# Second attention with another order of units, and tile 0 of the first batch beside the first searched unit

## What is computed

```python
# per batch, Sq = 512, 32 query heads of 16, 8 key heads
draft = jnp.einsum('bhqd,bhkd->bhqk', qr, kr)        # rotated queries and keys
draft = draft + jnp.where(causal_future, neg, 0.0)
num_remain = 128
_, draft_indices = jax.lax.top_k(draft, num_remain)  # each row keeps its 128 largest
# softmax over those that are kept, times the values, then the output projection
```

## Time and profile before

| | |
|---|---|
| median of 3 runs | 2259.57 us (2258.46 to 2261.43) |
| the profiled execution | 2258.43 us |
| its span | 2256.6 us |
| PE, DVE, ACT, POOL busy | 1860.4, 1500.8, 1181.4, 802.9 us |
| the second attention's first score | 1160.4 us |
| its last residual addition | 2029.7 us |

### The profile page before, as it was taken

How to read it: one execution, slowest core, us unless ns; L and a number is a source line. 1 busy time by engine, 2 the same in 40 slices (tenths; PEclk the granted TensorE clock), 3 DMA queues, 4 the chain that set the end, 5 groups by cost and what they waited for, 6 DMA issues and landing times. The chain is left out here.

```text
span 2256.6 us, 27824 instructions
## 1 busy us (share of the span) xinstructions
PE 1860.4 (82%) x8600; PEld 1331.2 (59%) x8600; DVE 1500.8 (67%) x3325; ACT 1181.4 (52%) x2969; POOL 802.9 (36%) x523
## 2 busy tenths in 40 slices
PE   5898999988999769999765777778777777777997
PEld 4777777777777648887652443333444333335885
DVE  3677777777777644555652788888788888723335
ACT  3556656566565432333326677876677676242221
POOL 3445445455453435565321111112311112123442
PEclk9999999999999979999775778879887888887998
DMA  4011111111110112221240000010000000001111
GB/s 159 25 53 60 65 67 43 52 59 71 60 47 21 61 56 102 94 84 56 98 105 17 15 15 15 15 29 11 18 15 15 15 15 15 0 0 52 51 42 51
DMA packets 48722, 104.11 MB, mean 46 GB/s; under 512 B 6672, under 2 KB 30864, under 8 KB 44432
## 3 DMA queue, kind: packets, MB, share of 16 engines
q1 hardware_dynamic: 48624, 102.95, 13.7%
HBM read 95.59 MB, written 7.34 MB: 46 GB/s over the span
## 5 line engine op out<-in xcount | busy, mean ns | idle before, releaser
L225 PE MATMUL PS<-XT,AR 128*128 128x512 f32 x2472 | 620.2, 406 | 25.9 <-POOL AR L833 12.3
L225 PE MATMUL PS<-AR 128*128 128x512 f32 (+2 forms) x2568 | 540.7, 365 | 24.8 <-POOL AR L342 13.2
L225 PEld LDWEIGHTS PS<-XT,AR 128*128 128x128 f32 x2472 | 471.3, 193 | 139.4 <-issue 16.7
L225 PEld LDWEIGHTS PS<-AR 128*128 128x128 f32 x2568 | 441.5, 192 | 117.8 <-POOL AR L342 16.2
L1436 POOL TENSOR_TENSOR AF<-AF 128x512 f32<-128x512 f32 (+3 forms) x64 | 148.4, 2320 | 675.0 <-DVE AF L1668 675.0
L1610 DVE MAX8 BF<-PS 128x8 f32<-128x256 f32 (+2 forms) x384 | 196.7, 555 | 60.7 <-PE PS L1233 59.1
L1376 ACT ACTIVATE AF<-PS 128x512 f32<-128x512 f32 x160 | 92.5, 595 | 268.6 <-PE PS L1244 191.5
L1258 PE MATMUL PS<-AF,BF 128*128 128x512 f32 x320 | 190.3, 699 | 28.8 <-ACT AF L1376 28.6
L586 POOL TENSOR_TENSOR AF<-AF 128x512 f32<-128x512 f32 (+1 forms) x64 | 107.5, 1680 | 169.2 <-DVE AF L717 169.2
L580 POOL TENSOR_TENSOR AF<-AF 128x512 f32<-128x512 f32 x80 | 103.3, 1292 | 169.3 <-ACT AF L372 169.3
L1212 PE MATMUL PS<-AR,XT 48*128 48x128 f32 (+3 forms) x256 | 94.9, 454 | 73.3 <-DVE BF L1538 40.7
(11 more groups left out here) (195 smaller groups left out, 3451.2 us busy)
## 6 DMA issues: line engine op xcount, KB each, us to landing
AF<-in_mean_w SPq DMA_DIRECT2D x48, 448.0 KB, 3.3
AF<-in_ffn_w SPq DMA_DIRECT2D x14, 1536.0 KB, 6.6
AF<-in_attn_w SPq DMA_DIRECT2D x9, 1536.0 KB, 8.1
XT<-rope_scratch SPq DMA_DIRECT2D x180, 64.0 KB, 2.8
AF<-in_attn_w SPq DMA_DIRECT2D x9, 1024.0 KB, 5.0
AF<-in_ffn_w SPq DMA_DIRECT2D x11, 769.0 KB, 4.2
rope_scratch<-BF SPq DMA_DIRECT2D x20, 256.0 KB, 2.3
AF<-in_x SPq DMA_DIRECT2D x8, 256.0 KB, 4.1
```

Of the source, the lines that this page charges most:

```text
L225: last = nc.tensor.matmul(dst, lhs(a, c), rhs(m, c), start=(first and k == 0), stop=(k == 3 * n - 1 and not more))
```

## The change

The order becomes `TILES1 = [0, 1, 2, 3, 7, 6, 5, 4]`, and tile 0 is no unit any more: units now begin with tile 1, so there are 14 of them (`n = x // 2 + 1`), and step x picks and counts what step x + 2 did. The two halves e = 0, 1 of tile 0 are done by functions of their own with buffers of their own: `Se[e]`, columns 256 to 511 of the second score buffer, and `qe[e]` for the queries. Exponentials are made in place in `Se` (L1454), and all 16 heads are normed by one instruction.

```diff
-        NB = 2 * TT
-        TILES1 = [0, 1, 2, 3, 5, 6, 7, 4]
+        NB = 2 * (TT - 1)
+        TILES1 = [0, 1, 2, 3, 7, 6, 5, 4]
...
+        Se = [S1[1][:, :, 256 + P * e:256 + P * (e + 1)] for e in range(2)]
+        qe = [XT2[0:48].rearrange("p (h k) -> p h k", h=16), AR1[0:48, 4096:6144].rearrange("p (h k) -> p h k", h=16)]
...
+            def extra_scores(e):
+                pe.wait_ge(A1["qste"], 16 * 12)
+                pe.wait_ge(A1[f"kst{e}"], 48)
+                for pair in range(8):
...
+            def extra_values(e, g):
+                if g == 0:
+                    pe.wait_ge(A1["pnorm"], e + 1)
+                if g < 4:
+                    tn = 4 * e + g
+                    wait(pe, A1["pt"], tn - 1)
+                    for h in range(G1):
+                        last = nc.tensor.transpose(PS[:, 4 + tn % 2, h * P:(h + 1) * P], Se[e][:, 4 * g + h, :], ident)
...
                     if 0 <= xp - 1 < NB and h <= tile_of(xp - 1)[1] + 1:
                         values(xp - 1, 3, h)
-                    if h == 12 and xp >= 1 and (xp - 1) % 2:
-                        project((xp - 1) // 2)
+                    if x == 1 and 4 <= h <= 8:
+                        extra_values(0, h - 4)
+                    if h == 12 and xp >= 2 and (xp - 1) % 2:
+                        project((xp - 1) // 2 + 1)
+                    if h == 12 and x == 2:
+                        project(0)
...
+                if x == 1:
+                    for g in range(5):
+                        extra_values(1, g)
...
+            def extra_exp(e):
+                act.wait_ge(A1["nmax"], 2)
+                for h in range(16):
+                    last = nc.scalar.activation(Se[e][:, h, :], Se[e][:, h, :], ACT.Exp, bias=nmax_e[:, e, h:h + 1],
+                                                scale=SCALE1, accum_out=rsum_e[:, e, h:h + 1])
+                last.then_inc(A1["exp"], 1)
...
                 if x >= 3 and x % 2:
...
-                if shown:
+                    o_hi((x - 3) // 2 + 1, tcount(x - 1, 0, 0))
+                if x == 1:
+                    extra_pt(0)
+                    extra_exp(1)
+                elif shown:
                     exp(xp, 0)
                 if search:
                     count(x, 1)
+                if x == 0:
+                    extra_exp(0)
+                if x == 1:
+                    exp(0, 0)
                 if shown:
                     exp(xp, 1)
+                if x == 1:
+                    extra_pt(1)
+                    o_hi(0, 8)
                 if search:
                     count(x, 2)
...
+                if x == -1:
+                    first_thresholds()
                 for q in range(4):
                     if 0 <= xp < NB:
                         final(xp, q)
                     if x + 1 < NB:
                         evac(x + 1, q)
+                    if x == 0 and q == 2:
+                        extra_rinv(0)
+                    if x == 1 and q == 1:
+                        o_lo(0)
                     if search and q == 2:
                         update(x, 2)
-                if x == -1:
-                    first_thresholds()
                 if x + 1 < NB:
                     start(x + 1)
+                if x == -1:
+                    extra_evac(0)
+                    extra_evac(1)
+                    extra_start()
+                    dve.wait_ge(A1["tiny"], 1)
+                    values_of(0)
```

More of the change, by code:

```diff
@@ L1238, in values @@
                 if kb == 0:
[L1239 removed]
+                    pe.wait_ge(A1["pnorm"], group(x, q))
                 if kb <= i:
@@ L1376, in pt, with extra_pt, o_hi @@
                     nc.scalar.activation(PT1[:, tn % 2, :], PS[:, 4 + tn % 2, :], ACT.Copy).then_inc(A1["pt"], 1)
+            def extra_exp(e):
[4 more added lines that the diff above has]
+                last.then_inc(A1["exp"], 1)
+            def extra_pt(e):
+                for tn in range(4 * e, 4 * e + 4):
+                    act.wait_ge(A1["turned"], tn + 1)
+                    wait(act, A1["pv"], tn - 1)
+                    nc.scalar.activation(PT1[:, tn % 2, :], PS[:, 4 + tn % 2, :], ACT.Copy).then_inc(A1["pt"], 1)
+            def o_hi(n, products):
+                act.wait_ge(A1["pv"], products)
+                wait(act, A1["yproj"], n)
+                nc.scalar.activation(OT1[:, 0], PS[:, 6, :].rearrange("p (h k) -> p h k", h=4), ACT.Copy)\
+                    .then_inc(A1["o_hi"], 1)
             for x in range(0, NB + 2):
```

183 lines of the change are left out of this document (122 added, 61 removed).

## The result

| | before | after |
|---|---|---|
| median of 4 runs each, one chip, us | 2260.5 (2258.5 to 2267.0) | 2232.2 (2229.4 to 2236.1) |
| profiled execution; its span | 2258.43; 2256.6 | 2229.73; 2227.9 |
| mean granted clock | 0.894 | 0.905 |
| first score of the second attention | 1160.4 | 1158.2 |

The ratio is 0.9867, its 95% interval 0.9844 to 0.9889: 28 us won, where 7.4 were forecast. That is outside the forecast's range and beyond rival A, its best case. Of the twelve executions of the kernel before that were timed beside the first four experiments, two took 3680 and 4351 us and are left out of its median there, 2260.8.

A forecast was written before the change was run, and what follows sets the result against it. Start and end were taken as latency, the searched steps as nearly all DVE's (76 to 80% busy). 9.0 - 3.5 - 0.8 + 2.7 = 7.4 us won gave a median of 2252.2, range 2245 to 2261.

The forecast's parts named there:

- rival A: Second attention: the copy finds the port free, PE has the upper clock for tile 0's blocks; 15.0 won, 2244.6; chance 0.14.
- The start: From the first score to the first searched unit's picks: these begin at 1216.4 instead of 1244.1, 27.7 us won.
- The copy: DVE's small scaling and copy of the values before the first update, beside POOL's negations: 3.2 taken, between 0.6 and 5.8.
- Rival D: DVE's threshold updates wait for POOL's negations and norm: 8.0 more, 0.6 lost, 2260.2; chance 0.06.
- Step 1: First searched unit's picks, with tile 0's value blocks, ACT's queue a chain: 72.5 long, ending at 1288.9, 9.0 won so far.
- eight heads, four turns, three products: PE's work early in step 1, priced at the lower clock: 20.4, taken as 19.5 since the clock may rise.
- the fifteen hand-overs: Hand-overs in step 1, a row showing 0.21 and others up to 0.4: 2.1 added.
- Order of batch 1: Tiles 7 6 5 4 for 5 6 7 4: saving of the step without counts about equal, wide evacuations mostly covered; 0.8 lost.
- Rival B: Order of tiles: the wide evacuations count in full, 6.4 instead of 0.8; 1.8 won, 2257.8; chance 0.20.
- The tail: End of the attention: two blocks instead of four ahead of the last but one projection, 6.0 to 3.3, 2.7 won.
- Step 2: Step picking a unit of 256, now also with tile 0's projection: 4.1 less 0.6 for a moved subtraction, 3.5 lost.
- Rival C: ACT's queue in step 1, with lower clock and no overlap: 13.8 more, 6.4 lost, 2266.0; chance 0.14.

The follow-up runs named there:

- the first four experiments: Against the kernel before: new order alone 2255.3; tile 0's move alone 2239.1; changed kernel with tiles 6 and 7 swapped 2240.9; with ACT's third counts moved earlier 2239.8.
- the second profile: The changed kernel run and profiled again with no edit, as a yardstick: 2233.2 us, ratio 0.9864 to the kernel before; step 1 took 64.8.
- the run for it: The changed kernel with tiles 6 and 7 changed over (0, 1, 2, 3, 6, 7, 5, 4): 2240.9 us, ratio 0.9895 to the kernel before.

## Why the prediction was wrong

**The start, 2.3 too little: the step "The copy".** It took 3.2 for scaling and copy beside POOL's negations, from one small scaling that had taken 2.31. Here the negations ran over the same instructions and these took 1.1 together. That was luck of the moment as much as a rule: the same copy beside the same negations took 0.41 here, 0.81 in the run with the thresholds put back and 1.22 in the one with the blocks ahead of the cut. Counts and exponentials were priced rightly. Rival D cost nothing in this kernel: the first update took 0.16 and 0.18 while POOL negated, and no norm ran beside the third. But its mechanism exists, and its "Against: no row shows such an operation stretched" was a matter of the rows chosen: in the kernel before, the third update's first operation, with two inputs in SBUF, took 2.38 in place of 0.17 beside a norm, and in the run with the thresholds put back the first update took 1.00 beside the negations. So the rule of the Trainium skill ("GPSIMD Engine Reference", "Specifications"), that VectorE instructions with two SBUF inputs contend, agrees with the norms in every step that picks 512, and with the negations only at times.

**Step 1, 8.6 too long (7.7 by the second profile): the lower clock.** Of it 5.8 lie between step's begin and cut, in the sum "eight heads, four turns, three products, 20.4; I take 19.5". Its durations were all of 0.50, for the whole stretch. (The sum then goes on at 1236.5, which is 20.1 behind the begin and not 19.5; the 0.6 between them is given no source.) The changed kernel had the clock up 10 to 11 us into the step. The run with 48 matmuls shows the size: with no lower clock 27.2, with some 11 us of it 30.9. Had it held for all 20 us, that rate gives about 34 (an estimate), so some 2 of the 5.8 are not the clock's. The remaining 2.8 (0.9 from cut to the third counts' end, 1.9 behind) were not traced to a cause; the fifteen hand-overs, added at 2.1, are as large. The chain itself was right: the blocks behind the cut took 7.0 (forecast 8), both waits that it named are there, and the runs that took one away met the next.

**The order, 9.8 too little: the step "Order of batch 1".** The view that failed is that the step without counts saves about the same for any width: at 256 it took 41.3 where the step ahead of it took 54.3, at 512 69.5 for 72.8, each pair differing by the counts and one projection: 13.0 against 3.3. I had compared only the widths, and not asked what DVE waits for in that step (8.4 for exponentials at 512, 3.4 at 256). The order as a whole gave 5.4 in the ten steps, where 0.8 was to be lost; how the 5.4 divide between the last step and the order of neighbours stays open, since the run for it also had another clock. And 3.6 were no part of the order: 3.2 of them are before's step of 76.0, which had the lower clock. Rival B (wide evacuations in full) did not occur: the two steps that it wanted near 80 and 75 took 72.8 and 71.2; the forecast's reason was right, and the rows show it: the hold by POOL's norm and the wait for exponentials shrank by the 4.3.

**The tail, 1.5 too much: the clock again.** Two blocks fewer were priced at PE's 2.7, and 2.6 were there: the next block of tile 4 was turned 13.4 behind the last step's end before and 10.8 here. Then 1.2 were lost at once, since PE did that block's turns and product at the lower clock (1.12 and 2.08 for 0.66 and 1.32), which leaves 1.4 at the last residual addition (41.9 behind the step's end, where "near 40.6" was forecast) and 1.2 at the program's end.

```profile
2001.19 1.32 PE L1258 MATMUL PS<-AF,BF 128*128 128x512 f32 x2 [0.74 <-ACT AF L1376]
```

```profile
1971.58 2.08 PE L1320 MATMUL PS<-AF,BF 128*128 128x512 f32 x2 [0.74 <-ACT AF L1448]
```

**Step 2, 3.5 forecast, 3.6 measured**: right in size; its terms were not taken apart.

Rival A had the right mechanism (copy not held, upper clock) at 7.6 of the 10.9 that were there, and nothing for the order. Rival C's mechanism, ACT's queue, exists and has its two waits; its price supposed the lower clock, which came in part. The range was too narrow since every case in it took the order as a loss.

## To carry to other kernels

Where four engines pass small work around, look for the long idle stretch of the engine whose product everything waits for: ACT's 16.2 us, filled by moving DVE's two small updates (and, with them, some exponentials on ACT), were worth 17 us, while reordering a queue in which PE, ACT and DVE alternate only moved a wait of 6 to 7 us from one to the next. Price a stretch of PE work at both clock levels and look at what PE does just ahead of it; a few unused matmuls that end at its first instruction may be worth more than a better order. And where the last step of such a loop lacks part of its work, ask what its engine will wait for instead: here the step saved more with the narrow tile in it.

## What had not been expected of the hardware

- The share of time in which PE is busy did not tell the clock. In the start it is busy 32.6 of 53.7 us at 0.50, with score matmuls of 48 rows and mask additions of 128 by 128, and in the version with early updates 32.7 of 36.5, still at 0.50:

```profile
1162.40:1198.90 36.50, 32.65 (x129) 20.39 (x129) 25.22 (x156) 33.32 (x137) 5.69 (x2) 0.50 0.38 108
```

  Eight back-to-back matmuls of 128 by 512 behind the same work, and the next 6 us had 0.93.
- The same steps of the same program, with DVE's work unchanged, took 60.4 or 63.4 and 72.8 or 76.6, with the granted clock at 0.89 or 0.84 and 0.88 or 0.82; an edit in step 1 was enough to change this in step 3.
- POOL's norms hold DVE. In the steps that pick 512 the small scaling of start() and the first operation of the third update last 1.2 to 2.9 us, where they take 0.17 or 0.18 alone, and each time they end 0.03 behind the norm.
- Beside POOL's negations it varies. In the kernel before, the small scaling (2.31) and the copy behind it (2.08) both lasted until the negation was over. Here the scaling took 0.88, and the copy ended while POOL was negating: 0.41, as later without it (0.42). What lets one pass and holds the other stays open.

```profile
1178.67 2.08 DVE L1704 COPY BF<-AF 128x512 f32<-128x512 f32 x1
```

  (the copy in the kernel before)
